# Keys as fp32 matmuls, and three of four batches of x transposed on the host, in a gated cross-attention and mixture kernel

## The reference

```python
def rmsnorm(x, w):
    var = mean(x * x, axis=-1, keepdims=True)
    return x * rsqrt(var + 1e-6) * w
# layer 1: cross-attention, added to x
t = layernorm(x)                                  # (x - mean) / sqrt(var + 1e-5)
F = rmsnorm(ctx, fn_w)
Q = rmsnorm(t @ Wq.T + bq, qn_w);  K = rmsnorm(F @ Wk.T + bk, kn_w)
x = x + tanh(g_xattn) * (softmax(Q @ K.T / sqrt(1024)) @ F)
# layer 2: a dense layer and eight gated low-rank experts (rank 16), added to x
z = layernorm(x)
gate = softmax(z @ W_gate.T);  thr = sigmoid(z @ W_thr + b_thr) / 8
w = relu(gate - thr), divided by its sum
x = x + tanh(g_ffn) * (z @ W_base.T + b_base + 2 * sum_e w_e * (z @ A_e.T) @ B_e)
```

## Time and profile before

| | us |
|---|---|
| median of 3 runs (525.88, 531.17, 530.93) | 530.93 |
| profiled execution: its time | 526.89 |
| profiled execution: span, first to last instruction | 525.1 |
| TensorE busy | 500.9 (95%) |
| VectorE busy | 271.2 (52%) |
| ScalarE busy | 153.0 (29%) |
| GpSimd busy | 153.4 (29%) |
| read from and written to memory | 34.67 and 8.39 MB |

### The profile page before, as it was taken

One profiled execution on the slowest core, in us unless ns is written; L12 is line 12 of the kernel. 1 busy time (PEld: TensorE's weight loads), 2 busy tenths in 40 slices (PEclk: granted clock), 3 DMA queues, 4 the chain that ended last, 5 costly groups with the idle time before them and its releaser, 6 DMA issues.

```text
span 525.1 us, 7062 instructions
## 1 busy us (share of the span) xinstructions
PE 500.9 (95%) x2768; PEld 459.6 (88%) x2768; DVE 271.2 (52%) x584; ACT 153.0 (29%) x323; POOL 153.4 (29%) x123
## 2 busy tenths in 40 slices
PE   2589999999999999999988999999999999999997
PEld 2589888888888888888888999999999999999997
DVE  3887543525352532156568766456554565654423
ACT  4476444243223322354541112211112111111100
POOL 3456566312222221145273320122201222012200
PEclk9799999999999999999999999999999999999999
DMA  8643611111112001321550322113221112210012
GB/s 316 256 157 114 240 41 41 41 41 40 41 40 81 1 1 64 139 71 51 201 161 32 90 80 81 41 40 122 80 81 52 41 69 81 82 41 38 3 41 81
DMA packets 11617, 43.51 MB, mean 83 GB/s; under 512 B 1600, under 2 KB 1984, under 8 KB 11200
## 3 DMA queue, kind: packets, MB, share of 16 engines
q1 hardware_dynamic: 11584, 43.06, 22.6%
HBM read 34.67 MB, written 8.39 MB: 82 GB/s over the span
## 4 chain that ended last, share of the span: by engine, by line
PE 81%; DVE 10%; DMA 3%; POOL 2%; ACT 2%; issue 2%; SPq 0%; POOLq 0%; DVEq 0%; ACTq 0%
PE bank L399 11%; PE bank L401 11%; PE bank L400 11%; PE bank L467 10%; PE bank L468 10%; PE bank L466 10%; PE bank L332 6%; DMA bb<-b_base_dram 2%; PE bank L480 2%; DVE xn L710 2%; DVE small L697 1%; PE bank L482 1%; PE bank L481 1%; PE bank L417 1%; PE bank L416 1%
## 5 line engine op out<-in xcount | busy, mean ns | idle before, releaser
L466 PE MATMUL bank<-wch,zth 128*128 128x388 f32 x384 | 132.5, 345 | 0.0
L467 PE MATMUL bank<-wcl,zth 128*128 128x388 f32 x384 | 130.5, 340 | 0.0
L468 PE MATMUL bank<-wch,ztl 128*128 128x388 f32 x384 | 129.8, 338 | 0.0
L399 PE MATMUL bank<-xth,wqh 128*128 128x512 f32 x256 | 102.1, 399 | 0.0
L401 PE MATMUL bank<-xth,wql 128*128 128x512 f32 x256 | 100.0, 390 | 0.0
L400 PE MATMUL bank<-xtl,wqh 128*128 128x512 f32 x256 | 99.8, 390 | 0.0
L899 POOL TENSOR_TENSOR small<-small,mhalf 128x1 f32<-128x1 f32 (+1 forms) x42 | 25.8, 615 | 218.8 <-DVE small L702 190.2
L773 DVE SCALAR_TENSOR_TENSOR qtl<-bank,vecs,qth 128x512 fp32r<-128x512 f32 x32 | 24.0, 750 | 100.5 <-ACT sq L630 100.5
L466 PEld LDWEIGHTS bank<-wch,zth 128*128 128x128 f32 x384 | 72.2, 188 | 1.0
L467 PEld LDWEIGHTS bank<-wcl,zth 128*128 128x128 f32 x384 | 72.3, 188 | 0.6
L468 PEld LDWEIGHTS bank<-wch,ztl 128*128 128x128 f32 x384 | 72.1, 188 | 0.0
(11 more groups left out here) (113 smaller groups left out, 642.3 us busy)
## 6 DMA issues: line engine op xcount, KB each, us to landing
x<-x_dram SPq DMA_DIRECT2D x32, 512.0 KB, 3.3
out_dram<-x SPq DMA_DIRECT2D x15, 512.0 KB, 2.6
wc_raw<-wc_dram SPq DMA_DIRECT2D x3, 1552.0 KB, 6.1
wk_raw<-wk_dram SPq DMA_DIRECT2D x8, 512.0 KB, 10.6
wq_raw<-wq_dram SPq DMA_DIRECT2D x8, 512.0 KB, 5.5
fn_raw<-ctx_dram SPq DMA_DIRECT2D x8, 256.0 KB, 5.0
ctx_raw<-ctx_dram SPq DMA_DIRECT2D x2, 512.0 KB, 3.7
fnw<-fn_w_dram SPq DMA_DIRECT2D x1, 512.0 KB, 6.4
```

What stands on the lines that cost most here:

```text
L399: pe.matmul(acc[:, :], wqh[f][:, k, :], xth[b % 2][:, k, :], start=k == 0, stop=False)
L466: pe.matmul(acc, zth[z][:, k, :], wch[c][:, k, :], start=k == 0, stop=False)
L467: pe.matmul(acc, zth[z][:, k, :], wcl[c][:, k, :], start=False, stop=False)
L468: done = pe.matmul(acc, ztl[z][:, k, :], wch[c][:, k, :], start=False, stop=k == KB - 1)
```

## The change

1. The context arrives transposed from the host (`ctxt`). Its 1024 feature rows are multiplied by fn_w in place, even column blocks on ScalarE and odd ones on VectorE, without the normalisation.
2. A key block is eight fp32 matmuls of the unsplit weights by the unsplit transposed context, into half a PSUM bank. The context's inverse root mean square is spread to all partitions by two transposes (`rsb`) after the first query block and multiplied in when a key block is evicted (`k_out`, now on VectorE).
3. k0 to k3 stand before the first query block, k4 and k5 after it, k6 and k7 after the second.
4. x of batch 0 is normalised and transposed as before, from four places of its own. x of batches 1 to 3 arrives transposed from the host (`xt`); the plain tiles are loaded too, for mean and variance (`x_stat`). TensorE spreads the batch's mean and inverse deviation over all partitions into two PSUM banks (`mr`, eight transposes), and VectorE subtracts and multiplies against these (`z`), ScalarE makes the high part (`zh`) and VectorE the low one (`zl`), in four pieces, during blocks 3 to 7 of the batch before.
5. The query weights' low parts are shared: even on GpSimd, odd on VectorE. The fn_w broadcast for the attention output moves from the start to before the last batch. SP's first issues are written out by hand, with two waits among them; the vectors are loaded from ScalarE's queue.

```diff
-        for f in range(FB):
-            if f + 3 < FB:
-                first.append(("wk", f + 3))
-            first.append(("k", f))
...
+        first = [("ct", 0), ("ct", 1), ("ct", 2), ("ct", 3), ("small",), ("k", 0), ("ln_stat", 0), ("ln", 0), ("k", 1),
+                 ("ln_stat", 1), ("ln_stat", 2), ("ln", 1), ("xt", 0, 0), ("xt", 0, 1), ("k", 2), ("ln", 2),
+                 ("ln_stat", 3), ("xt", 1, 0), ("xt", 1, 1), ("ln", 3), ("wq", 0), ("xt", 2, 0), ("xt", 2, 1), ("k", 3),
+                 ("xt", 3, 0), ("xt", 3, 1), ("ctx_norm",), ("wq", 1)]
         for b in range(B):
             for f in range(FB):
+                if b + 1 < B and f < 2:
+                    first += [("x_stat", (b + 1) * TPB + 2 * f + j) for j in range(2) if b > 0]
                 if b == 0 and f + 2 < FB:
                     first.append(("wq", f + 2))
+                if b + 1 < B and f >= 4:
+                    first.append(("zl", b + 1, f - 4))
+                if b + 1 < B and 3 <= f < 7:
+                    first.append(("z", b + 1, f - 3))
+                first.append(("q", b, f))
+                if b + 1 < B and 3 <= f < 7:
+                    first.append(("zh", b + 1, f - 3))
+                if b == f == 0:
+                    first += [("rsb",), ("k_out", 0), ("k_out", 1), ("k_low", 0), ("k_out", 2), ("k_low", 1), ("k_out", 3),
+                              ("k_low", 2), ("k_low", 3), ("x_stat", TPB), ("x_stat", TPB + 1)]
+                if b == 0 and f < 2:
+                    first += [("k", 2 * f + 4), ("k", 2 * f + 5)]
+                    first += [("x_stat", TPB + 2 + j) for j in range(2) if f == 1]
+                    first += [("k_out", 2 * f + 4), ("k_out", 2 * f + 5),
+                              ("k_low", 2 * f + 4), ("k_low", 2 * f + 5)]
...
                 if b + 1 < B:
-                    first += [("xt", (b + 1) * TPB + u // NH, u % NH) for u in XT_AT[f]]
+                    if f == 2:
+                        first.append(("mr", b + 1))
```

On TensorE:

```diff
+                if stage == "rsb":
+                    acc = ring_open((stage,), "act")
+                    pe.wait_ge(g_const, CONSTS)
+                    pe.wait_ge(g_ctx, 1)
+                    transposes(acc, ctx_rs.unsqueeze(2).to_broadcast([P, 2, P]))
+                elif stage == "mr":
+                    b, = i
+                    pe.wait_ge(g_mr, b)
...
+                    for k, n_bank in enumerate((M_BANK, S_BANKS[b % 2])):
+                        for j in range(TPB):
+                            done = pe.transpose(bank[n_bank][:, j * P:(j + 1) * P],
+                                                ms[b % 2][:, k, j:j + 1].to_broadcast([P, P]), ident[:, :])
+                    done.then_inc(p_mr, 1)
...
                     for k in range(KB):
-                        pe.matmul(acc, wkh[f][:, k, :], fth[:, k, :], start=k == 0, stop=False)
-                        pe.matmul(acc, wkh[f][:, k, :], ftl[:, k, :], start=False, stop=False)
-                        done = pe.matmul(acc, wkl[f][:, k, :], fth[:, k, :], start=False, stop=k == KB - 1)
+                        if f == 0:
+                            if k % 4 == 0:
+                                pe.wait_ge((ld_wk[0], ld_wk0)[k // 4], 16)
+                            pe.wait_ge((a_ct, v_ct)[k % 2], k // 2 + 1)
+                        done = pe.matmul(k_at(f), wkf[f][:, k, :], ct[:, k, :], start=k == 0, stop=k == KB - 1)
                     done.then_inc(p_k, 1)
...
-                    if n < 3:
-                        pe.wait_ge(a_kfull, FB + n - 2)
-                    else:
+                    if n in (1, 2):
+                        pe.wait_ge(v_kr, 2 * n)
+                    elif n > 2:
                         pe.wait_ge(v_qtl, n - 2)
...
                     for k in range(KB):
+                        if b > 0 and f == 0 and k % CK == 0:
+                            pe.wait_ge(v_zl, 4 * (b - 1) + k // CK + 1)
```

On SP (`load_x` of tiles 0 to 3 goes to four places in the query weights' region, which wq6 and wq7 take over; `load_xt` is four transfers of 512 KB):

```diff
+            load_ct(0)
+            sp.dma_start(wkf[0][:, 0:4, :], wk[0][:, 0:4, :]).then_inc(ld_wk[0], 16)
+            sp.dma_start(wkf[0][:, 4:8, :], wk[0][:, 4:8, :]).then_inc(ld_wk0, 16)
+            load_ct(1)
+            load_ct(2)
+            load_ct(3)
+            load_x(0)
+            load_wk(1)
+            load_x(1)
+            load_wk(2)
+            load_x(2)
+            load_x(3)
+            load_wq(0)
+            load_wk(3)
+            load_ctx(0)
+            load_ctx(1)
+            load_wq(1)
+            load_wk(4)
+            load_wk(5)
+            load_wq(2)
+            load_wk(6)
+            load_wk(7)
+            load_wq(3)
+            load_x(TPB)
+            load_x(TPB + 1)
+            load_wq(4)
+            load_wq(5)
+            sp.dma_start(sc[:, 0:3], scal.to_broadcast([P, 3])).then_inc(ld_sc, 16)
+            sp.wait_ge(v_xn, 4)
+            load_wq(6)
+            load_wq(7)
+            sp.wait_ge(p_k, 4)
+            load_xt(1)
...
+                elif stage == "q" and 0 < i[0] < B - 1 and i[1] == 0:
+                    b, f = i
+                    sp.wait_ge(p_q, nq(b, 0))
+                    load_xt(b + 1)
                 elif stage == "load_fn":
                     b, = i
+                    if b == 0:
+                        sp.wait_ge(v_z, 4 * (B - 1))
+                        sp.dma_start(fnw[:, :], fn_w.to_broadcast([P, D])).then_inc(ld_fnw, 16)
```

On VectorE (the halves on ScalarE are `zh`, a copy to fp32r, and for `k_out` the square and the high part):

```diff
+                elif stage == "x_stat":
...
+                    dve.wait_ge(ld_x[t % NXA], 16 * (n // NXA + 1))
+                    for h in range(NH):
+                        done = dve.bn_stats(x_stats[n % 2][:, 6 * h:6 * h + 6], xs[t % NXA][:, h * HALF:(h + 1) * HALF])
...
+                elif stage == "z":
+                    b, c = i
+                    n = 4 * (b - 1) + c + 1
+                    z = xt_raw[b % 2][:, CK * c:CK * c + CK, :]
+                    m, r = (bank[k][:, :].unsqueeze(1).to_broadcast([P, CK, TB]) for k in (M_BANK, S_BANKS[b % 2]))
+                    if c == 0:
+                        dve.wait_ge(p_mr, b)
+                    dve.wait_ge(ld_xt[c], 16 * b)
+                    dve.tensor_tensor(z, z, m, ALU.subtract).then_inc(v_zc, 1)
+                    dve.wait_ge(v_zc, n)
+                    dve.tensor_tensor(z, z, r, ALU.mult).then_inc(v_z, 1)
+                elif stage == "zl":
+                    b, c = i
+                    kc = slice(CK * c, CK * c + CK)
+                    dve.wait_ge(a_zh, 4 * (b - 1) + c + 1)
+                    dve.tensor_tensor(xtl[b % 2][:, kc, :], xt_raw[b % 2][:, kc, :], xth[b % 2][:, kc, :].bitcast(F32),
+                                      ALU.subtract).then_inc(v_zl, 1)
...
+                elif stage == "k_out":
+                    f, = i
+                    dve.wait_ge(p_k, 2 * (f // 2) + 2)
...
+                    dve.tensor_tensor(kr[f % 2][:, :], k_at(f), rsb[:, :], ALU.mult).then_inc(v_kr, 1)
+                    dve.wait_ge(v_kr, f + 1)
...
+                    dve.tensor_scalar(kfull[f % 2][:, :], kr[f % 2][:, :], kw[:, f:f + 1], kwb[:, f:f + 1], ALU.mult,
+                                      ALU.add).then_inc(v_kfull, 1)
```

More of the change, by code:

```diff
@@ L127, in build @@
         xs = [at(f"x{i}", [P, D], F32, o) for i, o in enumerate(x_at)]
+        xfirst = [at(f"xfirst{i}", [P, D], F32, r_wq + (12 + i) * ROW) for i in range(TPB)]
         xn = [at(f"xn{i}", [P, D], F32, r_xn + i * ROW) for i in range(2)]
@@ L155, in build @@
         mhalf = own("mhalf", [P, TPB])
-        vecs = own("vecs", [P, 4, FB])
+        vecs = own("vecs", [P, 5, FB])
         kw = own("kw", [P, FB])
@@ L199, in build @@
[L199 to L203, removed]
@@ L214, in build @@
-        for f in range(FB):
-            if f + 3 < FB:
-                first.append(("wk", f + 3))
-            first.append(("k", f))
[L218 to L226, removed]
+        (a_ct, a_ctx, a_tanh, a_high, a_ksq, a_kth, a_zh, a_wq, a_q, a_qsq, a_st, a_fnsq, a_fnh,
+         a_wc, a_hg, a_ex, a_bt) = (sem(f"a_{n}") for n in ("ct", "ctx", "tanh", "high", "ksq", "kth", "zh", "wq", "q", "qsq", "st", "fnsq", "fnh", "wc", "hg",
+                                                            "ex", "bt"))
@@ L236, in build @@
+                if b == 0 and f == 2:
+                    first.append(("tanh",))
+                if b == 0 and f == 4:
+                    first.append(("k_norm",))
                 if f > 0:
@@ L316, in build, with k_at @@
         WC_POOL = {(0, 0): 1, (0, 1): 2, (0, 2): 3, (0, 3): 4, (2, 2): 5, (2, 3): 6}
+        WQ_POOL = (0, 2, 4, 6)
+        WQ_LOW = {f: (g_wq if f in WQ_POOL else v_wq, f // 2 + 1) for f in range(FB)}
         WC_FREE = [nq(B - 2, FB - 1) + 1, nq(B - 1, 3) + 1, nq(B - 1, 6) + 1]
+        def k_at(f):
+            return bank[K_BANKS[f // 2]][:, (f % 2) * S_ALL:(f % 2 + 1) * S_ALL]
         ring = Ring()
@@ L381, in tensor @@
                         for half in range(2):
-                            done = pe.matmul(bank[KSQ_BANK][half * S:(half + 1) * S, 2 * b:2 * b + 2],
```

(29 more changed lines are left out.)

347 lines of the change are left out of this document (180 added, 167 removed).

## The result

The changed kernel takes 511.0 us (median of 4 runs, 510.1 to 511.7), beside 528.4 us before (4 runs, 525.6 to 531.2): a ratio of 0.967, 95% interval 0.960 to 0.974. The forecast was 511. The profiled execution took 511.14 us with a span of 509.4, where the sum of the prediction had 508.1.

What follows compares the result with a forecast made beforehand. TensorE, busy 500.9 of 525.1 us, was taken as the bound. First query at 25.9 us plus 482.2 us behind it gave a 508.1 us span; with 1.8 around it 509.9, median put at 511 us, range 503 to 519.

Steps and rivals of the forecast that it cites:

- The frame: Whole kernel: only when the first query starts and how much TensorE work stands behind that start move the end.
- The start: Before the first query matmul: it starts at 25.9 us instead of 49.7, a gain of 23.8 us.
- The order of the chains: Before the first query: TensorE's chain ends later, at 25.9 us; VectorE's lies close, not done before 22.2 us.
- The fp32 price: Key blocks: one fp32 matmul with 256 moving columns costs 0.456 us, two operations of 0.228; eight take 3.65 us.
- B: Rival, key blocks: the fp32 matmul costs only its lower bound, 0.24 us, giving 501 us; chance 0.10.
- Work behind the start: From the first query on: fewer x transposes, added key matmuls and spreading transposes, +6.8 us, so 475.4 becomes 482.2 us.
- What must stay hidden: Beside TensorE's query work: VectorE's x work (21.0 of a batch's 48 us), evictions and transfers cost nothing.
- a whole key pair stands behind the waits for kr: Early query blocks: 7.3 us of TensorE key work covers the context scale's eviction, copy and VectorE work.
- E: Rival, VectorE's queue: z, low parts and key evictions delay queries' low halves, 2 us per batch, 516 us; chance 0.07.
- C: Rival, colder or hungrier start: 16 more early key matmuls at the lower clock, 7.3 us, 517 us; chance 0.18.
- D: Rival, all 64 key matmuls: TensorE loses its upper clock under fp32, 29 us, 539 us, slower; chance 0.05.
- The number: Whole kernel: the sum gave 509.9 us; the median was put a little above it, 511 us; chance 0.60.

Runs made afterwards that it cites:

- warm: Changed kernel with ten idle fp32 identity matmuls on TensorE before the first key block: 513.2 us, ratio 0.971 to the kernel before.
- keys_first: Changed kernel with key blocks k4 to k7 also ahead of the first query block: 520.3 us, ratio 0.987 to the kernel before.
- keys_evicted: Changed kernel with k4 to k7, the context scale's spread and all key evictions ahead of the first query's eviction: 516.6 us, ratio 0.980.
- z_extra3: Changed kernel with three more VectorE operations per z piece, 36 in all, results unused: 529.3 us, ratio 1.003 to the kernel before.
- z_extra1: Changed kernel with one more VectorE operation of 1.2 us per z piece, 12 in all, result unused: 513.6 us, ratio 0.974.
- fnw_first: Changed kernel with the fn_w broadcast back at the head of SP's queue: 511.8 us, ratio 0.970 to the kernel before.
- bias_later: Changed kernel with the scaling of b_base and the first two bias additions behind the gates of tile 0: 508.9 us, ratio 0.965.
- start_fix: Changed kernel with early table load, ten idle TensorE matmuls, x3's transposes inside k3, and GpSimd's wq0 split held until x3 is normalised: 508.7 us.

## Why the prediction was right

By its own steps:

- **The frame**, TensorE's start and TensorE's work behind it: it held. That the two terms add up to the span proves nothing, since they cut it in two. What shows it is that each moved as it was costed, and that the transposes, put back, returned 10.5 us behind the first query where 10.6 were expected.
- **The start**, 25.9 forecast, 28.5 measured. Size off by 2.6: the first key matmul came 2.3 us late. I had allowed 0.5 us for scaling a column block, which took 0.52, and nothing for the vectors, which land at 4.86 us, or for the table load of 1.28. The first 5 us moved 0.75 MB, not the 2 MB per 5 us of later, and x tile 0 landed at 10.5, not 8.1. The order of the chains was right: TensorE's set the start in the profile. VectorE's is close enough behind that a flip of order makes it the later one (warm).
- **The fp32 price**, 0.456 forecast, 0.433 measured (3.46 us per block of eight): B is out. There are two array operations per matmul, 0.216 us each, close to the 0.228 of a 512-column fp32r matmul, as the argument on two parts times two had it. That is 4 x 0.108 us for 256 columns, and it agrees with the four passes that the Trainium skill names (FP8 and Floating Point Precision, TensorE Precision Notes). The price by four passes was put at 0.48, because 0.12 us, the distance of fp32r matmuls, stood for one of them.
- **Work behind the start**, 482.2 forecast, 480.9 measured: 32 x 0.023 = 0.7 less for the keys, and 0.9 less waiting in the output stage, which the sum had left alone.
- **What must stay hidden** stayed hidden: z took 1.21 and 1.22 us, the low parts 1.47 in the median, forecast 1.3 each; VectorE stood once for ScalarE, 0.3 us. The line "a whole key pair stands behind the waits for kr" was the right cover and a dear one: without it 6 to 9 us go. E was priced too low. Three more operations make 2.4 us for each of the three of a piece (3.0 for each of the two z operations) and already cost 18 us, which takes back the whole gain, while I had put that point at 3.4 without a working that can be followed. I priced waits and not the clock that falls after some of them, 5 us here.
- **C and D**: only k0 and part of k1 ran at half the pace, together 9.4 us against two times 3.46; the sum had 9.1 for them, so C is out. The low stretch of the kernel before, which I had read as 5 us, is 6.6 us by its 0.67 over 10 us. With key block behind key block at 1.00 from 23 to 41 us in keys_first, and k4 to k7 at 0.433 in the changed kernel, D is out.
- **The number.** Start 2.6 later, work 1.3 less: the sum was 1.3 us below the span. The 1 us that I put on top for the median happened to meet it, and its reason was wrong: the kernel's median and its profiled execution differ by 0.1 us, not by 4. That 511 met 511.0 is luck: two errors of opposite sign, and an allowance that covered what they left.

In part open: why the kernel before spreads over 8 us (524.6 to 532.5 over all runs here) and the changed one over 1.6. The granted clock goes a part of the way. Its mean was 0.987 to 0.994 in 36 of the 37 executions of the kernel before that were timed beside the experiments and 0.999 to 1.00 in all four of the changed one; before, the four at 0.987 took 529.9 to 532.5 us and the one at 1.00 took 526.5. But three at 0.992 took 524.6 to 525.1, so it isn't all. Whether keys and evictions could be ordered without interleaving at no cost wasn't tried beyond keys_evicted. And the parts of the change were not undone one by one: what leaving out the context's normalising and splitting gives, and what the fn_w broadcast, is known only together.

## What to carry to other kernels

When one engine is busy nearly throughout, price a change as its start plus the work behind the start; everything else costs only where its cover goes. Work with no consumer nearby (here key blocks) is good cover for an eviction queue, so ask what an early, dense stage would leave uncovered before moving it out of the way. A gain made early must be followed to the end of the trace: two of these edits gained at the start or in the middle and lost it at one wait 200 us later. A wait of a few microseconds can be paid twice, once as time and once as clock, but not each is: in these traces most waits of 2.5 us and more were, and most shorter ones were not.

## What the runs showed of the hardware

- A fp32 matmul of 128 x 128 weights by 256 columns is two array operations and 0.433 us; the three fp32r products took 0.36. Over all eight key blocks that is 4.7 us more of TensorE time.
- After a wait the granted clock can fall to 0.50 for a few microseconds, which cost 1.7 us or 3.4 us each time. Of the twelve waits of TensorE of 2.5 to 4.1 us after its first work, in all fourteen traces, ten had such a stretch beside or behind them; in the kernel before (2.55 us in the output stage) and in keys_first (2.9 us there) the clock stayed at 1.00. Of the seventeen of 1.5 to 2.2 us four had one, all in z_extra3. The same two waits before the first query (0.9 and 1.5 us) were followed by a fall that cost 3.4 us in z_extra3 and by none in z_extra1, fnw_first, warm and bias_later.
- Some VectorE operations stretch beside a running GpSimd operation, even tiny ones: normalising an x tile took 0.80 us or 2.63, a 128 x 8 operation with two scalars per partition 0.29 or 1.66, a 128 x 1 operation with two tensor operands 0.16 or 2.11. The last two end with GpSimd's operation, within 0.1 us. Two reciprocals and a scaling by constants beside the same operation did not stretch (0.15 to 0.16 us each, at 255.2 to 255.4 us of the changed kernel), nor did those that read PSUM (L778, 0.64 us each beside GpSimd's split of the output weights at 250 us).
- ScalarE's table load (1.28 us) stands behind the first activation's wait, at 4.9 us in the changed kernel. In start_fix an earlier idle activation moves it to 1.2 us.
